# TensorE's small per-pair products, taken in groups with turns, projection and output products between them

## The reference

```python
for i in range(6):
    x = attn_layer(shift_tokens(x), Wqkv[i], ..., Wo[i]) + x
    x = ffn_layer(shift_tokens(x), ...) + x
# attn_layer: 16 heads of 64, windows of 32 queries
q, k, v = split(x @ Wqkv)                        # 128 -> 3 * 1024
q = rotary(l2norm(q) * qs); k = rotary(l2norm(k) * ks)
sim = einsum('bhwie,bhwje->bhwij', bq, bk2) * 8  # 32 queries x 64 keys
attn = softmax(where(mask, -max, sim))
out = einsum('bhwij,bhwje->bhwie', attn, bv2)    # (32 x 64) @ (64 x 64)
return out @ Wo                                  # 1024 -> 128
```

## Time and profile before

| | |
|---|---|
| median of 3 runs | 3935.38 us (3933.94 to 3938.61) |
| the profiled execution | 3928.65 us, span 3926.6 us |
| TensorE matmul | 3690.6 us busy, 94% of the span, 67712 records |
| TensorE weight load | 2844.7 us, 72% |
| VectorE, GpSimd, ScalarE | 3058.0 us (78%), 2597.4 us (66%), 2270.7 us (58%) |
| TensorE's granted clock | 0.986 of full speed over the execution |

### The profile page before, as it was taken

The page is one execution under the profiler, slowest core; times in us unless marked ns, Lnnn a source line. Parts: engine busy times, 40 slices in busy tenths (PEclk is TensorE's granted clock), DMA queues, the critical chain, the costliest instruction groups (busy, mean ns, idle before and its releaser), DMA issues.

```text
span 3926.6 us, 163773 instructions
## 1 busy us (share of the span) xinstructions
PE 3690.6 (94%) x67712; PEld 2844.7 (72%) x67712; DVE 3058.0 (78%) x5829; ACT 2270.7 (58%) x4270; POOL 2597.4 (66%) x3029
## 2 busy tenths in 40 slices
PE   5999979999999999999999999999999999999998
PEld 3555557777767777677877678787677876777876
DVE  7666658888778888788887788887788887888876
ACT  3555546666546666456666366665466664566653
POOL 4545538787547887367887288775477873687870
PEclk8999989999999999999999999999999999999999
DMA  1000002222212222122222122222122221222220
GB/s 44 4 6 4 6 28 68 56 60 60 58 32 59 59 57 59 41 49 60 61 57 56 30 65 57 59 61 58 32 60 58 59 56 41 54 57 58 60 52 22
DMA packets 136313, 189.08 MB, mean 48 GB/s; under 512 B 38006, under 2 KB 58484, under 8 KB 135412
## 3 DMA queue, kind: packets, MB, share of 16 engines
q1 hardware_dynamic: 135540, 178.23, 17.7%
HBM read 22.67 MB, written 2.10 MB: 6 GB/s over the span
## 4 chain that ended last, share of the span: by engine, by line
PE 76%; issue 4%; DVE 2%; POOL 2%; ACT 0%; DMA 0%; POOLq 0%; SPq 0%; DVEq 0%; ACTq 0%
PE PS L1270 18%; PE PS L1417 10%; PE PS L1256 10%; PE PS L1294 8%; PE PS L1280 8%; PE PS L1258 8%; PE PS L1257 8%; PE PS L1476 2%; PE PS L1411 2%; PE PS L1454 1%; PE PS L1447 1%; POOL t L1182 1%; PE PS L1442 1%; POOL t L1187 0%; DVE m L1800 0%
## 5 line engine op out<-in xcount | busy, mean ns | idle before, releaser
L1182 POOL TENSOR_TENSOR t<-t 128x1024 f32<-128x1024 f32 x384 | 908.0, 2370 | 363.9 <-DVE t L1762 362.6
L1187 POOL TENSOR_TENSOR t<-t,rn 128x1024 f32<-128x1024 f32 x384 | 723.6, 1905 | 29.8 <-POOL rn L150 27.3
L1542 ACT ACTIVATE va<-PS 128x512 f32<-128x512 f32 x384 | 229.8, 599 | 614.4 <-PE PS L1258 611.6
L1760 DVE TENSOR_TENSOR t<-PS,rope 128x512 f32<-128x512 f32 x768 | 523.2, 681 | 26.1 <-ACT sq L1577 24.5
L1256 PE MATMUL PS<-w_hi,xh 128*128 128x512 f32 x1152 | 514.2, 446 | 22.3 <-DVE xl L1063 11.3
L1577 ACT ACTIVATE sq<-PS 128x512 f32<-128x512 f32 x768 | 454.1, 593 | 33.0 <-PE PS L1258 17.7
L1270 PE MATMUL PS<-constants,t 128*128 128x128 f32 x3072 | 443.8, 277 | 19.8 <-POOL t L1187 12.8
L1258 PE MATMUL PS<-w_lo,xh 128*128 128x512 f32 x1152 | 458.5, 398 | 0.0
L1257 PE MATMUL PS<-w_hi,xl 128*128 128x512 f32 x1152 | 457.5, 397 | 0.0
L1767 DVE TENSOR_REDUCE ss<-sq 128x16 f32<-128x1024 f32 x384 | 448.3, 1209 | 0.0
L1270 PEld LDWEIGHTS PS<-constants,t 128*128 128x128 f32 x3072 | 351.9, 141 | 68.9 <-POOL t L1187 15.9
(11 more groups left out here) (168 smaller groups left out, 7869.8 us busy)
## 6 DMA issues: line engine op xcount, KB each, us to landing
vs<-va SPq DMA_DIRECT2D x768, 130.0 KB
vs<-va SPq DMA_DIRECT2D x768, 65.0 KB
t<-in_L_ffn_Wqkv SPq DMA_DIRECT2D x18, 512.0 KB, 4.4
w_out<-in_L_ffn_Wo SPq DMA_DIRECT2D x6, 512.0 KB, 3.9
a_normed<-in_L_attn_x SPq DMA_DIRECT2D x8, 256.0 KB, 7.0
a_xo<-in_L_attn_x SPq DMA_DIRECT2D x8, 256.0 KB, 2.8
out<-total SPq DMA_DIRECT2D x8, 256.0 KB, 3.5
w_raw<-in_L_ffn_W SPq DMA_DIRECT2D x6, 341.0 KB
```

What stands on the lines that cost most here:

```text
L1182: pool.tensor_tensor(mine[:, i, :], mine[:, i, :], t2[:, i, :], ALU.add).then_inc(done, 1)
L1187: pool.tensor_tensor(h, h, bc(rn[:, H * i:H * (i + 1)], 2, HB), ALU.mult).then_inc(done, 1)
L1760: dve.tensor_tensor(o1, src, bc(rope[:, 2 * i, t, :], 1, 8), ALU.mult)
```

## The change

Only TensorE's order inside a slot changes; every product, wait and signal is still there, and no other engine's queue is touched. Three places:

- `mix_and_turn_q` replaces `mix_half(0)` and the first four turns of q where both are in the slot: pairs 0 and 1, a turn, pair 2, a turn, pair 3, two turns.
- `mix_and_project_v` replaces `mix_half(1)` and the v chunk: pairs 4 and 5, a projection product, pair 6, a product, pair 7, a product.
- `score_half(1, output_pairs)` puts two output products ahead of each of its four pairs, instead of all eight ahead of the four pairs.

```diff
+                def mix_and_turn_q():
+                    pe.wait_ge(pT_made, at(T, 2, 2, 1))
+                    pe.sem_inc(pv_begun, 1)
+                    mix_values(s2, tile2, (0, 1))
+                    wait_q(0)
+                    turn_block(4, 0, roped(0))
+                    mix_values(s2, tile2, (2,))
+                    turn_block(4, 1, roped(0))
+                    mix_values(s2, tile2, (3,)).then_inc(pv_mm, 1)
+                    turn_block(4, 2, roped(0))
+                    turn_block(4, 3, roped(0)).then_inc(qt_mm, 1)
+                def mix_and_project_v():
+                    pe.wait_ge(pT_made, at(T, 2, 2, 2))
+                    pe.sem_inc(pv_begun, 1)
+                    mix_values(s2, tile2, (4, 5))
+                    pe.wait_ge(rq_made, at(T, 0, 2, 1))
+                    project_part(0, 2, 1, 6, t)
+                    mix_values(s2, tile2, (6,))
+                    project_part(1, 2, 1, 6, t)
+                    mix_values(s2, tile2, (7,)).then_inc(pv_mm, 1)
+                    project_part(2, 2, 1, 6, t).then_inc(v_mm, 1)
...
-                    return score_pairs(tile1, range(4 * c, 4 * (c + 1)))
+                    for n in range(4):
+                        if between is not None:
+                            between(n)
+                        last = score_pairs(tile1, (4 * c + n,))
+                    return last
...
+                if mix and score:
+                    mix_and_turn_q()
+                elif mix:
                     mix_half(0)
+                else:
+                    turn_q(0)
                 if score:
-                    turn_q(0)
                     turn_q(1)
-                if mix:
+                if mix and project_new:
+                    mix_and_project_v()
+                elif mix:
                     mix_half(1)
...
-                    for pair in range(PAIRS):
+
+                def output_pairs(n):
+                    for pair in (2 * n, 2 * n + 1):
                         last = pe.matmul(PS[:, y_at, 0:P], w_out[:, pair, :], oT[:, pair, :],
-                                         start=(pair == 0), stop=(pair == PAIRS - 1))
-                    last.then_inc(y_mm, 1)
+                                         start=(pair == 0), stop=(pair == PAIRS - 1), skip_group_check=True)
+                    if n == PAIRS // 2 - 1:
+                        last.then_inc(y_mm, 1)
+
                 if score:
-                    score_half(1).then_inc(s_mm, 1)
+                    score_half(1, output_pairs if mix else None).then_inc(s_mm, 1)
+                else:
+                    for n in range(PAIRS // 2):
+                        output_pairs(n)
```

More of the change, by code:

```diff
@@ L1258, in split_matmul, with project_part, turn_block @@
                 return pe.matmul(out, hi, w_lo, start=False, stop=True)
+            def project_part(n, i, c, bank, t):
+                cols = slice(INNER * i + 512 * c, INNER * i + 512 * (c + 1))
+                left, right = ((xh, w_hi), (xl, w_hi), (xh, w_lo))[n]
+                return pe.matmul(PS[:, bank, :], left[:, P * t:P * (t + 1)], right[:, cols], start=(n == 0), stop=(n == 2))
             def project(i, c, bank, t, done):
-                cols = slice(INNER * i + 512 * c, INNER * i + 512 * (c + 1))
-                split_matmul(PS[:, bank, :], xh[:, P * t:P * (t + 1)], xl[:, P * t:P * (t + 1)],
-                             w_hi[:, cols], w_lo[:, cols]).then_inc(done, 1)
+                for n in range(3):
+                    last = project_part(n, i, c, bank, t)
+                last.then_inc(done, 1)
+            def turn_block(bank, j, source):
+                return pe.transpose(PS[:, bank, P * j:P * (j + 1)], source(j), ident)
             def turn(bank, source, done):
                 for j in range(4):
-                    last = pe.transpose(PS[:, bank, P * j:P * (j + 1)], source(j), ident)
+                    last = turn_block(bank, j, source)
                 last.then_inc(done, 1)
@@ L1284, in score_pairs, with mix_values @@
                 return last
-            def mix_values(s, t, c, done):
-                for pair in range(4 * c, 4 * (c + 1)):
+            def mix_values(s, t, pairs):
+                for pair in pairs:
+                    c = pair // 4
                     for par in range(2):
@@ L1296, in mix_values @@
                                              skip_group_check=True)
-                last.then_inc(done, 1)
+                return last
             def slot(lay, s, t, ages):
@@ L1315, in turn_weights, with wait_q @@
                     turn(2 + c, lambda j: pw[:, 4 * c + j, :, :].rearrange("p r k -> p (r k)"), pt_mm)
-                def turn_q(c):
+                def wait_q(c):
                     pe.wait_ge(qn_made, at(T, 1, 1, 1))
@@ L1320, in turn_q @@
                         pe.wait_ge(rk_made, at(T, 0, 2, c + 1))
+                def turn_q(c):
+                    wait_q(c)
                     turn(4 + c, lambda j: roped(0)(4 * c + j), qt_mm)
+                def mix_and_turn_q():
[19 more added lines that the diff above has]
+                    project_part(2, 2, 1, 6, t).then_inc(v_mm, 1)
                 def turn_k(c):
@@ L1337, in mix_half, with score_half @@
                     pe.sem_inc(pv_begun, 1)
-                    mix_values(s2, tile2, c, pv_mm)
-                def score_half(c):
+                    mix_values(s2, tile2, range(4 * c, 4 * (c + 1))).then_inc(pv_mm, 1)
+                def score_half(c, between=None):
                     pe.wait_ge(carried, at(T, 1, 1, 1))
```

1 line of the change is left out of this document (removed).

## The result

The changed kernel takes 4238.3 us (median of 4 runs, 4232.8 to 4241.5) against 3935.3 (4 runs, 3933.9 to 3938.6): the ratio is 1.0767, with a 95% interval of 1.0749 to 1.0786. It is 303 us slower; 4218 us were forecast for it. Its profiled execution took 4232.8 us, its span 4231.0, with a granted clock of 0.983.

The account below looks back on a forecast made before the run. It took TensorE's own queue as the bound (94% busy). Profiled 3928.65 + 340 (full slots) + 8 (closing slots) - 65 (waits back) = 4212 us; with 6.7 for the median of runs, 4218; range 4100 to 4295.

Parts of the forecast that it names:

- The passage: TensorE going from full products to small ones and back pays some 0.3 us each time, whatever the groups' length.
- The division of the cost of leaving: Extra 0.16 us of a row of turns between small products: 0.06 at the first product, 0.10 at the last.
- The lone projection product: In the v chunk, a single projection product between small ones: 0.42 us with leaving, middle of bounds 0.32 and 0.53.
- The sum per slot: Added TensorE time per full slot: q turns 0.46, v chunk 0.52, output products and scores 0.91, together 1.89 us.
- What came back: Waits for late instruction packets on TensorE's small products, 97 us, shrink behind the new delays: 65 us taken back.
- Waits that could appear: Three possible new waits: state addition before VectorE's maximum, mix turns behind VectorE's division, q turns and v chunk; cost 0.
- it fits by 0.15: Second turns of the mix come 1.34 us after the last small start, VectorE's division ends at 1.19: no wait.
- cost of all three: 0: State addition, turns of the mix behind the division, and timing of q turns and v chunk add no waiting time.
- The cover of the addition to the state: VectorE's addition ends at +0.61, the maximum behind it starts at +0.72: hidden by 0.1 us; uncovered, at most 54 us.
- The gain without pauses: Rival, chance 0.08: pauses are not paid again, late instructions are the limit; 72 and 97 us saved, 3767 us.
- Half the pauses: Rival, chance 0.12: first full product after a short small group pays no 0.06 to 0.10; 112 us less, 4106.
- VectorE's chain: Rival, chance 0.07: `y_mm` and `s_mm` close together hold up VectorE's maximum by the whole addition; 54 us more, 4272.

Follow-up runs that it names:

- The experiment with full and small products at the same places: Kernel before plus three needless products in the first half of the mixed values, one behind each of pairs 0, 1, 2: full 4054.2 us, small 3981.4 us.
- the needless products: Kernel before plus three needless full products (identity turns), one behind each of pairs 0, 1 and 2 of the mixed values: 4054.2 us, ratio 1.0297.
- the output products alone: Only the third place changed against the kernel before, two output products ahead of each pair of the second score half: 4067.2 us, ratio 1.0342.

## Why the prediction was right

*The passage.* The step that carried it held to 0.01 us: a lone turn 0.41 (0.147 + 0.258 by the medians), eight small products in 0.13, four output records 0.64. The division of the cost of leaving, which no row had shown, held too: a row's last turn stands 0.203 ahead of the small products and a lone one, which is first and last at once, 0.258, so 0.055 is the first one's part (forecast 0.06). The lone projection product stands 0.426 ahead (forecast 0.42); that the middle between the two bounds was right is luck. The experiment with full and small products at the same places shows that it is the change of shape that costs.

*The sum per slot.* Forecast 0.46 + 0.52 + 0.91 = 1.89. Measured by the medians of the pieces: 0.45, 0.60 and 0.93. The first is within 0.01. The second is larger by the wait for the division (0.07), the third by 0.07 for the wait on turned k, less a few hundredths (the first of the four groups takes 0.61, the small ones with their end 0.27 for 0.28). The third is from first score to next projection, 4.49 for the 3.56 of the earlier trace rows. In time: 0.447 x 186 + 0.603 x 180 + 0.93 x 186 = 365 us; forecast 348.

*What came back.* Forecast 65 us, measured 98 - 30 = 68. 365 - 68 = 297, and the difference of the runs is 303. That this term came so close is partly luck: with the needless products I made the same estimate by the same reasoning, took 40 us and found 82, and for the output products alone 10 and 48.

*Waits that could appear.* This is the step that was off. I reckoned for the turns of the mix that "it fits by 0.15": VectorE began its reciprocal 0.33 after the last small start and not 0.25, and the handing over of the signal was not in the sum. And I said of the three waits "cost of all three: 0" without asking behind which other waits the output products now stand: the kernel shows it, `between(n)` is called below the waits of `score_half`. Each of the two waits costs 0.07 us a slot. With the few hundredths the other way this is the 17 us between 348 and 365; less the 3 more that came back, it is 14 of the 20 us between 4218 and 4238. The cover of the addition to the state held, with the reason given.

A term that the sum did not have is the clock, which was to stay at its full level in the slots: 0.983 were granted for 0.986, and the surplus at the lower level, counted as above, is 40 us for 25. That is more than the 6 us still missing, so here too the parts are not exact to 10 us.

*The rivals.* The gain without pauses (3767) is excluded by every run that added full groups between small ones: all were slower than the kernel before. "Half the pauses" is excluded by the lone turn: the first full product after only eight small ones, with instructions at hand, is as late as after 32 (0.147 us by the medians), and as dear. VectorE's chain did not lengthen: the weights' turns stand 0.43 us behind the last projection product before and after, by the medians.

## What to carry to other kernels

Before small products are put between full ones, count the added passages and price one from the distances between starts, since busy time hides it: here some 0.3 us each, and seven more in a slot cost 7.7%. Where long rows of small products wait for instructions instead, move full work between the small runs that are there already and leave the number of passages alone: one such order was 1.1% faster here. Where a step is moved into a function, look at which waits it now stands behind.

## What the runs showed of the hardware

Products of the small shape (64 rows, 32 columns) start 0.007 to 0.008 us apart for the first sixteen of a row, and within 0.01 us of a needless one of the same shape. The step from them to a full product took 0.15 us by the medians in every kernel run here where nothing else was waited for, and the step back 0.20 us from the last of a row of full turns or output products, whatever the groups' length. A lone turn adds 0.055 to that.

TensorE's instructions arrive 256 at a time, and a wait for them ended some 1.4 us behind a packet's landing. Where a row of small products used them up, it waited up to 2.7 us at a time, at places that are fixed in the stored program: 16 products in front of a loop moved the grid by 31 records, and 32 of them made a kernel slower by 43 us (1.2%) that was otherwise the same. A comparison of two orders that differ by 1% can be this alone.
